# Scattering the expert lists slot by slot in a routed feed-forward layer: order and waits of 128 small indirect DMAs

## The reference

```python
full_logits = x @ gate_w.T                      # 8 routed experts and 1 shared
mult, sel = _sparse_mixer(dyn_logits)           # TOP_K = 4 picks a token, with weights
slot_valid = jnp.arange(TOP_K)[None, :] < dyn_k[:, None]
mult = jnp.where(slot_valid, mult, 0.0)         # dyn_k: picks needed for 0.75 of the probability
...
cap = 640                                       # ceil(4096 / 8 * 1.25)
mask_dyn = mask_dyn * (jnp.cumsum(mask_dyn, axis=0) <= cap)
...
out = sum over e of global_w[t, e] * down_e(silu(gate_e x) * up_e x)   # 8 routed, width 256
out = out + global_w[t, 8] * shared(x)                                 # 1 shared, width 1024
```

## Time and profile before

| what | value |
|---|---|
| device time, median of 3 runs (lowest, highest) | 1249.32 us (1249.26, 1250.52) |
| the profiled execution: span, first to last instruction | 1257.6 us |
| its own time beyond that span | none is given |
| instructions | 29419 |
| TensorE matmul busy | 1189.3 us, 95% of the span |
| VectorE, ScalarE, GpSimd busy | 950.4, 708.7, 589.7 us |
| mean granted TensorE clock | 0.990 |

### The profile page before, as it was taken

The page is one execution under the profiler, slowest core; times in us unless marked ns, Lnnn a source line. Parts: engine busy times, 40 slices in busy tenths (PEclk is TensorE's granted clock), DMA queues, the critical chain, the costliest instruction groups (busy, mean ns, idle before and its releaser), DMA issues.

```text
span 1257.6 us, 29419 instructions
## 1 busy us (share of the span) xinstructions
PE 1189.3 (95%) x10692; PEld 822.8 (65%) x10692; DVE 950.4 (76%) x2006; ACT 708.7 (56%) x1988; POOL 589.7 (47%) x685
## 2 busy tenths in 40 slices
PE   6888998799999999999999999999999998799996
PEld 3555665588888888786444445777777776466663
DVE  5889898899999999896677777777777775445460
ACT  4377788799899999896344322222222231365552
POOL 0047668737666667733200000445544345466744
PEclk9999999999999999999999999999999999899999
DMA  9522033134445454643870141221314320799987
GB/s 346 210 60 76 1 32 46 43 111 142 165 135 169 159 172 148 181 157 119 153 196 1 41 127 34 68 44 60 69 34 108 96 68 2 220 254 242 256 139 96
DMA packets 157567, 150.28 MB, mean 119 GB/s; under 512 B 78544, under 2 KB 111472, under 8 KB 157424
## 3 DMA queue, kind: packets, MB, share of 16 engines
q1 hardware_dynamic: 139584, 125.94, 35.5%
q0 software_dynamic: 13248, 21.15, 8.9%
q10 hardware_dynamic: 4592, 1.32, 0.6%
HBM read 84.93 MB, written 57.19 MB: 113 GB/s over the span
## 4 chain that ended last, share of the span: by engine, by line
PE 59%; DMA 17%; issue 8%; DVE 8%; POOL 5%; ACT 3%; ACTq 0%; SPq 0%; POOLq 0%; DVEq 0%
PE bank L121 28%; DMA lists<-att_land 14%; PE bank L1503 6%; PE bank L2125 5%; PE bank L955 4%; POOL lists L1629 4%; PE bank L1435 4%; PE bank L1456 3%; PE bank L1450 2%; PE bank L1421 2%; DMA q_rows<-att_land 1%; PE bank L1024 1%; ACT att_land L1353 1%; PE bank L872 1%; PE bank L891 1%
## 5 line engine op out<-in xcount | busy, mean ns | idle before, releaser
L1629 POOL DMA_INDIRECT lists<-att_land x128 | 134.4, 1050 | 310.7 <-DVE att_land L1770 166.8
L1353 ACT ACTIVATE att_land<-bank,att_land 128x120 f32<-128x120 f32 x512 | 178.3, 375 | 11.3 <-DVE att_land L1221 11.2
L2125 PE MATMUL bank<-att_land 128*128 128x512 f16 x768 | 177.3, 381 | 0.6 <-DVE program_logits L1304 0.6
L1952 ACT ACTIVATE att_land<-program_x 128x512 f32<-128x512 f32 x40 | 25.2, 631 | 195.2 <-DVE program_x L2094 165.1
L2125 PEld LDWEIGHTS bank<-att_land 128*128 128x128 f16 x768 | 75.4, 98 | 82.9 <-issue 2.0
L121 PE MATMUL bank<-program_xs,program_wgu 128*128 128x512 f16 x576 | 128.7, 379 | 0.6 <-DVE att_land L1729 0.6
L1353 ACT ACTIVATION_READ_ACCUMULATOR att_land<-bank,att_land 128x1 f32 x512 | 112.8, 221 | 0.0
L121 PE MATMUL bank<-att_land 128*128 128x128 f16 (+1 forms) x1560 | 101.0, 221 | 0.5 <-DVE att_land L1278 0.5
L121 PEld LDWEIGHTS bank<-program_xs,program_wgu 128*128 128x128 f16 x576 | 56.2, 98 | 67.5 <-DVE att_land L1729 1.1
L1221 DVE TENSOR_REDUCE att_land<-bank 128x4 f32<-128x480 f32 x128 | 82.4, 644 | 20.5 <-PE bank L1421 20.1
L1503 PE MATMUL bank<-att_land 128*128 128x512 f16 x384 | 93.4, 379 | 0.0
(11 more groups left out here) (305 smaller groups left out, 2817.2 us busy)
## 6 DMA issues: line engine op xcount, KB each, us to landing
att_land<-q_rows SPq DMA_DIRECT2D x96, 128.0 KB, 2.6
xn_rows<-att_land SPq DMA_DIRECT2D x37, 256.0 KB, 3.7
out_rows<-att_land SPq DMA_DIRECT2D x37, 256.0 KB, 6.4
q_rows<-att_land SPq DMA_DIRECT2D x32, 256.0 KB, 2.9
xt_tiles<-att_land SPq DMA_DIRECT2D x32, 256.0 KB, 2.1
x_rows<-program_x SPq DMA_DIRECT2D x8, 1024.0 KB, 4.8
att_land<-x_rows SPq DMA_DIRECT2D x8, 1024.0 KB, 5.6
program_xs<-xt_tiles SPq DMA_DIRECT2D x28, 256.0 KB
```

The costliest lines, as they stand in the source:

```text
L1353: last = act.activation(prob[:, c, h, :], ps_s[c % 2][:, h, :], ACT.Exp, bias=nmax[:, u % 2, c, h:h + 1], accum_out=rsum[:, u % 2, n:n + 1])
L1629: pool.indirect_dma_start(out=io["lists"], out_offset=bass.IndirectOffsetOnAxis(ap=index[:, t, k:k + 1], axis=0), in_=load[:, t, k, :], in ...
L2125: last = pe.matmul(ps_y[i][:, :], hid[:, c % 2, a, i * P:(i + 1) * P], wd[:, q, c, :], start=c == 0 and n == 0, stop=c == NC - 1 and n == 2)
```

## The change

The scatters are reordered: all 32 token tiles of slot 0 first, then all of slot 1, 2 and 3. `lists` is now raised four times, once a slot, by the slot's last instruction (the sum that writes the weights), and GpSimd waits for step k + 1 ahead of slot k's first scatter. The token numbers of all four slots are written to `load` by one copy ahead of the loop, in place of one copy a slot, and the copy that raised `lists` is gone. VectorE waits for `lists` where `link` had it wait for its own semaphore. The wait for scatter n - 2, the DMAs and their number stay.

```diff
         def scatter(pool, io):
 
-            need(pool, lists, 1)
             for n in range(NT * TOPK):
-                t, k = divmod(n, TOPK)
+                k, t = divmod(n, NT)
+                if t == 0:
+                    need(pool, lists, k + 1)
                 need(pool, listed[n % 2], 16 * (n // 2))
...
             link(tt(slot[:, :, :], slot[:, :, :], kept[:, :, :], ALU.mult))
+            link(dve.tensor_copy(load[:, :, :, 0], token[:, :, 0:1].to_broadcast([P, NT, TOPK])))
             for k in range(TOPK):
                 yield
                 link(tt(eq[:, :, :], oh[k][:, :, :], slot[:, :, :], ALU.mult))
                 link(reduce(sk[:, :, :], eq[:, :, :], AX.X, ALU.add))
                 link(ts(index[:, :, k:k + 1], sk[:, :, :], OFF, None, ALU.add))
                 link(tt(eq[:, :, :], oh[k][:, :, :], wgt[:, :, :], ALU.mult))
-                link(reduce(load[:, :, k, 1:2].bitcast(f32), eq[:, :, :], AX.X, ALU.add))
-                link(dve.tensor_copy(load[:, :, k, 0:1], token[:, :, :]))
-            dve.tensor_copy(sk[:, :, :], sk[:, :, :]).then_inc(lists.handle, 1)
+                reduce(load[:, :, k, 1:2].bitcast(f32), eq[:, :, :], AX.X, ALU.add).then_inc(lists.handle, 1)
+                need(dve, lists, k + 1)
             yield
```

## The result

The changed kernel is a little slower, not faster: median 1257.67 us in 20 runs (1247.84 to 1270.32), beside 1251.80 us in 20 runs of the kernel before on the same chip (1248.09 to 1255.38). The ratio is 1.0044, 95% interval 1.0026 to 1.0062. The changed kernel's runs also spread more, over 22 us in place of 7. Its recorded execution took 1257.64 us, with a span of 1255.9; the later runs have both numbers too, and the time is the span + 1.7 to 1.8 us (2.0 in e1 and e1b). By that the kernel before's recorded execution, span 1257.6, took some 1259.3 us, longer than every one of its 20 runs. The record doesn't name its chip.

The account below looks back on a forecast made before the run. TensorE's 12.5 us wait for expert 0's gathered rows, behind GpSimd's 128 scatters, was taken as the bound. Join -14.3, next wait 0 to +0.5, rest 0: -14.2 from 1249.3 gives 1235.1 us, range 1234.0 to 1245.5.

Parts of the forecast that it names:

- I carry the difference over: 1249.3 - 14.2: Final sum: the 14.2 us saved in the recorded span comes off the median too, giving 1235.1 us.
- Rival A: The wait for gathered rows is shorter unrecorded, 4.4 us, gain 5.9: 1243.4 us, or between 1236 and 1246; chance 0.24.
- rival B: Unrecorded runs don't wait for the rows, or something else holds the join too: within 0.2%, 1249 us; chance 0.08.
- longest idle shown: GpSimd's longest idle before a scatter, 3.60 us, with 0.97 of issue a 4.57 us step, used for the pace's upper bound.
- whether scatters slow VectorE's line 1963: VectorE's two-operand line took 692 ns before any scatter and 682 ns among them, so scatters don't slow it.
- First scatter: GpSimd's first scatter waits for slot 0 alone and starts at 745.25, 36.03 us earlier than before.
- Later slots' waits, VectorE's copy: Waits for later slots cost nothing; one added VectorE copy in unit 16, about 0.3 us, is covered by TensorE's work.
- Pace: GpSimd's 127 scatter steps stay at 2.180 us each, 276.87 in all, within 199 to 353; last start 1022.1.
- Join: Where TensorE waited for expert 0's rows: 14.3 us gained, 12.7 wait and 1.58 clock; next wait 0 to 0.5.
- the limit of 2.364 us a step: Slowest mean scatter pace, 8% above 2.180, at which the rows still arrive before TensorE is free at 1063.94.
- Rival C: Slot 0's full scatters back to back hinder each other; loss above 3.3 us a step, up to 1289 us; chance 0.04.
- The lock: Skill's rule: VectorE and GpSimd hold a shared port in turn, so early scatters meet VectorE's busiest stretch; no loss expected.

Follow-up runs that it names:

- e1: Changed kernel with the 96 scatters of slots 1 to 3 left out, chip 14: 1245.31 us, ratio 0.9998 to the kernel before.
- e1b: Changed kernel with the scatters of slots 1 to 3 left out, once more, on chip 11: 1249.93 us, ratio 0.9989 to the kernel before.
- e2: Changed kernel, but the first scatter waits for all four slots as before, chip 14: 1246.23 us, ratio 1.0003 to the kernel before.
- b1: The kernel before, unchanged, recorded once more on chip 11: 1252.73 us, ratio 1.0009.
- a3: The changed kernel, unchanged, run again on chip 0: 1246.14 us, ratio 1.0005 to the kernel before.
- a4: The changed kernel, unchanged, run again on chip 3: 1247.78 us, ratio 0.9998 to the kernel before.
- e6: Changed kernel with slot 0's scatters, then slot 3's near-empty ones three times, slots 1 and 2 left out: 1.0006 on chip 0, 0.9993 on chip 3.
- e7: Changed kernel with slot 0's full scatters four times, slots 1 to 3 left out: 1.0029 on chip 0, 1.0016 on chip 3.
- e7b: Changed kernel with slot 0's full scatters four times, slots 1 to 3 left out, chip 0: 1248.55 us, ratio 1.0029, 2.380 us a scatter.
- e7c: Changed kernel with slot 0's full scatters four times, slots 1 to 3 left out, chip 3: 1248.42 us, ratio 1.0016, 2.347 us a scatter.
- e4: Changed kernel with only one scatter in flight in slots 2 and 3, so the lists come late, chip 14: 1292.05 us, ratio 1.0364.
- e5: Changed kernel with the ten gathers of experts 0 and 1 held back by some 40 us, chip 11: 1251.45 us, ratio 1.0013.
- e6d: Changed kernel with slot 0's scatters, then slot 3's near-empty ones three times, slots 1 and 2 left out, chip 13: 1253.36 us, ratio 1.0016.
- a5: The changed kernel, unchanged, run again on chip 13: 1250.81 us, ratio 1.0016 to the kernel before.
- a1: The changed kernel, unchanged, run again on chip 11: 1253.65 us, ratio 1.0028 to the kernel before.
- e2b: Changed kernel, but the first scatter waits for all four slots as before, chip 3: 1245.72 us, ratio 0.999.
- e3: Changed kernel, but only 16 tiles of slot 0 early, the rest tile by tile as before, chip 14: 1246.59 us, ratio 1.0003.

## Why the prediction was wrong

**The failed step is the last one of the sum: "I carry the difference over: 1249.3 - 14.2".** The wait of 12.5 us belonged to one execution, the recorded one, and it was taken off a median that doesn't hold it. The warning stood in the text: a recorded span 8.3 us over the median, against a wait of 12.7. Rival A used it, but let the wait shrink by 8.3 only; rival B, that the rows aren't what usual runs wait for, got 0.08 and is what chips 0 and 3 show, and e1 and e2 on chip 14. By a limit of 2.080 us a step, which was there to be worked out from the rows, a pace 5% below the recorded 2.180 leaves no wait at all, and b1's was 6% below. The trace of before even held the surplus, in two steps that the prediction didn't look at (its "longest idle shown" was 3.60):

```profile
980.42 0.97 POOL L1629 DMA_INDIRECT lists<-att_land  x1 [8.48 <-DMA lists<-att_land]
...
1035.43 0.97 POOL L1629 DMA_INDIRECT lists<-att_land  x1 [6.65 <-issue]
```

The two steps took 9.45 and 7.62 us; no other recording has more than 7.4. The other 125 make 2.078 a step, just under the limit: without these two there is no wait. The Trainium skill, page "Runtime: NRT & Kernel Launch", preamble breakdown, would put some 6.2 us between the profile's total and the execution time; here the time lies above the recorded span, by 1.7 to 2.0 us in every run, so the 8.3 us were no fixed cost of recording but belonged to that execution.

**The second miss is a term that wasn't in the sum**: what GpSimd's issuing does to the steps that the other engines wait for. I had asked only whether scatters slow VectorE's line 1963 (692 and 682 ns) and put the rest at nothing. In the changed kernel's recording 11.3 us went there. That is why even the forecast for the recorded execution failed, 1255.9 against a span of 1243.4, though the join did what was said: -14.3 and +11.3 are -3.0, and +1.1 comes ahead of the first silu (785.28, before 784.18): -1.9, of the -1.7 seen. On chips without losses the changed kernel's spans are 1243.8 (a3) and 1242.5 (a4), beside 1243.4.

The other steps:
- **First scatter** 746.34, forecast 745.25. VectorE's last needed instruction ended at 745.40 in this execution, 1.1 later; the 0.94 from there held.
- **Later slots' waits, VectorE's copy**: nothing, as forecast (VectorE busy 26.26 of 37 us, before 26.74).
- **Pace**: mis-sized on the safe side. Taken as 2.180, it measured 1.881; 127 steps of it are 238.9 us, between the bounds of 199 and 353. The steps of slots 1 to 3 have a median near 1.6 us but a mean of 1.7 to 1.9, because waits of up to 4.3 us for a landing lie between them, and it makes no difference whether a scatter writes some rows or next to none (slots 1 and 3; e6). Full ones take 2.2 to 2.5 in the mean (e1, e7).
- **Join**: right. 6.06 us from the transposes to the first products, `down(63)` hidden, clock 1.00. e7b and e7c lie on the two sides of the limit of 2.364 us a step; that two single recordings bracket it so closely is luck.
- **Rival C** had the right sign and the wrong place. Full scatters back to back stay at 2.2 to 2.5 us a step in the mean, far from its 3.3, and the slowdown wasn't in the lists.
- **The lock** of the Trainium skill, page "SBUF — State Buffer", section on its two separate sides, isn't seen in what was looked at: VectorE's instructions keep their lengths beside scatters (0.42 us in the fences above) and start late because TensorE's products come late. But the page gives the lock to VectorE's two-port copies and casts, and for two operands in SBUF only against a GpSimd instruction that reads SBUF; line 1963, on which the prediction tested it, was no strong test, and no run here isolates the copies.

**Shown and not shown.** Shown: usual runs of before have no wait worth more than 0.2 to 0.3% to win back, on chips 14 and 11 (e1, e2, b1, e1b; on the result's chip it wasn't tested); late lists do reach the join (e4, e7b); the slowdown is 0.44, 0.28 and 0.16% on three chips (the last with an interval that touches 1.0) and none that can be measured on two; the lost time of the recordings lies in the units; the gathers' part moves with the gathers (831 to 844 in e1b, 998 to 1011 at first, 1041 to 1053 in e5, 1050 to 1062 in b1); and on three chips the steps of the other engines come late beside GpSimd's DMAs and nowhere else (961 of 4967 against 0 of 1911). Only argued: that the new order costs more because its later scatters come denser. Against a simple dose stand e6's ratios of 1 on chips 0 and 3, e6d's ratio, equal to a5's, and a1's lost time, equal to b1's, each from one recording. What differs between the chips, and by what path a GpSimd DMA delays a completion, stays open. No order tried beats the kernel before: e2b is nearest, at 0.999 (0.9977 to 1.0002).

## What to carry to other kernels

Before a wait in a recording is counted as a gain, hold the recorded time against the spread of the usual runs, and work out how little must change for the wait to be gone; if 5% of pace is enough, it may belong to the recording alone. The quickest test of what a side path can give is a run that leaves most of it out (e1): it named the floor in one run. Look, too, for single long steps in a chain before taking its mean. And an engine that isn't on the critical path is not free to be moved to where it is denser: compare the rhythm of the main loop with and without it, on more than one chip.

## What was unexpected of the hardware

- A pace of the same 128 scatters in the same order between 2.049 and 2.180 us a step from one execution to another, 17 us in all.
- One scatter in flight in place of two, for near-empty ones: e4's slots 2 and 3 took 3.6 and 3.3 us a step, against 1.7 to 2.0.
- Completions of TensorE, VectorE and ScalarE late beside GpSimd's DMAs, on three chips of six only: 483 of 4967 by over 1 us, in a loop whose units take 7.17 to 7.29 us in the twelve recordings of the other chips; the largest took 13.03.
- After a stall of 2.00 us TensorE ran 18 matmuls in 3.53 us, not 2.13, at a granted clock of 0.63 from 944 to 948.
- A spread that has nothing to do with the change: five recordings (a1, e1b, e2b, e3, e7c), of mean clock 0.990 to 0.992, have two stretches at half clock between 215 and 247 us, long before the routing. The stretch from 212 to 224 us of e2b and of a4:

```profile
212.00:224.00 12.00, 9.13 (x83) 6.67 (x81) 10.55 (x31) 7.38 (x16) 8.63 (x14) 0.72 0.09 17
```

```profile
212.00:224.00 12.00, 9.09 (x105) 6.92 (x104) 11.64 (x30) 8.62 (x18) 10.07 (x17) 1.00 0.15 34
```

Their spans are 1246.2 and 1242.5 us. The first silu starts at 787.50 and 783.48: all of the difference is made before the first silu.
